# Performer query walk: key sums as stationary weights in 32-column groups, quotient made on channels

## The reference, cut to what matters

```python
qkv = x @ W_qkv                                   # q, k, v: (B, 12, 548, 16)
qf  = features(q, proj_mat, is_query=True)        # (B, 12, 548, 44)
kf  = features(k, proj_mat, is_query=False)
# features: ratio * (exp(dash - diag - stab) + 1e-4)
out = (qf @ (kf.T @ v)) / (qf @ kf.sum(tokens))   # numerator / denominator
h   = h + out @ W_proj + b_proj
```

## Time and profile before

| | us |
|---|---|
| median of 3 executions | 4794.83 |
| lowest, highest | 4787.97, 4799.33 |
| profiled execution, its own time | 4788.87 |
| span of the profiled execution | 4787.1 |
| granted TensorE clock, mean over the span | 0.977 |
| query walk, first product to last addition to X | 375.64 to 760.08 |

### The profile page before, as it was taken

One profiled execution on the slowest core, in us unless ns is written; L12 is line 12 of the kernel. 1 busy time (PEld: TensorE's weight loads), 2 busy tenths in 40 slices (PEclk: granted clock), 3 DMA queues, 4 the chain that ended last, 5 costly groups with the idle time before them and its releaser, 6 DMA issues. The chain is left out here.

```text
span 4787.1 us, 139366 instructions
## 1 busy us (share of the span) xinstructions
PE 4643.0 (97%) x57372; PEld 3836.4 (80%) x57372; DVE 2459.5 (51%) x7361; ACT 2203.3 (46%) x5115; POOL 1544.6 (32%) x2385
## 2 busy tenths in 40 slices
PE   6999998999979999999999999999999999899999
PEld 4667775666658888888888888888888888799998
DVE  5655554666645554555555455555545544352332
ACT  3443442555545555554554455455445445222444
POOL 1000002666643333333333333333333333000555
PEclk8999997999989999999999999999999999999999
DMA  4111110000000000000000000000000000232333
GB/s 107 22 36 40 37 29 6 1 1 2 1 13 2 13 2 13 20 13 2 13 13 2 13 13 13 2 13 13 2 13 13 13 2 13 66 90 71 64 66 55
DMA packets 123860, 110.63 MB, mean 23 GB/s; under 512 B 65480, under 2 KB 111901, under 8 KB 123237
## 3 DMA queue, kind: packets, MB, share of 16 engines
q1 hardware_dynamic: 96081, 66.76, 6.0%
q0 software_dynamic: 16528, 23.16, 2.7%
q10 hardware_dynamic: 10628, 11.80, 1.1%
HBM read 59.76 MB, written 41.48 MB: 21 GB/s over the span
## 5 line engine op out<-in xcount | busy, mean ns | idle before, releaser
L2139 PE MATMUL PS<-th_kT,th_qg 64*125 64x274 f32 x10560 | 1416.8, 400 | 0.0
L1856 POOL TENSOR_TENSOR th_qg<-th_qT,w_th_th 128x180 f32<-128x180 f32 x1760 | 848.0, 504 | 1629.8 <-PE PS L2139 1620.5
L2044 ACT ACTIVATE th_P<-PS 110x600 f32<-110x600 f32 x880 | 647.6, 736 | 1113.3 <-PE PS L2126 1113.3
L1962 DVE TENSOR_REDUCE th_nmx<-PS 125x1 f32<-125x548 f32 x880 | 641.2, 729 | 902.3 <-PE PS L2139 902.3
L2126 PEld LDWEIGHTS PS<-th_mixn,th_P 61*110 61x110 f32 x17600 | 979.6, 173 | 103.2 <-issue 25.0
L2139 PEld LDWEIGHTS PS<-th_kT,th_qg 64*125 64x125 f32 x10560 | 938.2, 184 | 142.5 <-issue 0.2
L2126 PE MATMUL PS<-th_mixn,th_P 61*110 61x60 f32 x17600 | 975.6, 254 | 2.1 <-ACT th_P L2044 1.8
L2054 ACT ACTIVATE th_P<-PS,th_nb 125x548 f32<-125x548 f32 x880 | 621.8, 707 | 106.7 <-DVE th_nb L1965 106.7
L1317 POOL TENSOR_SCALAR ga_P<-ga_P,ga_rw 110x110 f32<-110x110 f32 (+4 forms) x240 | 265.5, 1118 | 199.7 <-DVE ga_rw L1483 196.0
L2161 PEld LDWEIGHTS PS<-th_P,th_v 110*32 110x32 f32 x11520 | 245.5, 115 | 29.9 <-issue 28.9
L2161 PE MATMUL PS<-th_P,th_v 110*32 110x90 f32 (+1 forms) x11520 | 266.4, 253 | 2.2 <-issue 1.3
(11 more groups left out here) (345 smaller groups left out, 6318.3 us busy)
## 6 DMA issues: line engine op xcount, KB each, us to landing
pf_xT<-pf_spill SPq DMA_DIRECT2D x32, 412.5 KB, 5.4
ex_tokens<-th_xn SPq DMA_DIRECT2D x128, 82.5 KB
pf_spill<-pf_xT SPq DMA_DIRECT2D x16, 412.5 KB, 3.7
ex_turned<-th_rT SPq DMA_DIRECT2D x16, 412.5 KB, 3.1
ex_x<-ex_turned SPq DMA_DIRECT2D x32, 206.2 KB, 4.0
out_h<-X SPq DMA_DIRECT2D x16, 330.0 KB
ex_w<-in_L_ffn_W ACTq DMA_DIRECT2D x18, 288.0 KB
ex_w<-in_L_ffn_W ACTq DMA_DIRECT2D x8, 576.0 KB
```

The source lines that it names most:

```text
L1856: ins = pool.tensor_tensor(qg[:, m % SB, :, 64 * s:64 * s + HQ].rearrange("p c (h n) -> p c h n", n=QH), qT[:, im % 2, :, at + s * QH:at + ...
L1962: dve.tensor_reduce(nmx[:, p:p + 1], PS[0:MR, bank:bank + 2, 0:HK], AX.XY, ALU.max, negate=True) \
L2044: act.activation(P2[:, :, :, at * QT:(at + 1) * QT].rearrange("p t h (s n) -> p s (t h) n", s=2), PS[0:R, MB:MB + 2, 0:VO].rearrange("p s ...
L2139: ins = pe.matmul(PS[0:MR, bank + a, 0:HK], qg[s, p, c, 0:MR], kT[s, im % 2, c, :], start=c == 0, stop=c == NC - 1)
```

## The change

`numerators` now uses the key sums as stationary weights and the features `fT` as moving data. The sums are kept in two tiles: `kvn` (2 heads x 16 channels = 32 columns for each pair of heads, the numerators) and `kvd` (32 columns as well: the denominator column of each head repeated 16 times). A product has 32 weight columns and 110 moving columns and writes 32 partitions of the bank, group `g` of the columns of the array writing partitions 32g to 32g + 31. So numerators and denominators come out with channels on partitions and tokens on columns. `divide` makes the reciprocal of all repeated denominators (128 x 110 and 64 x 110) and multiplies them with the numerators, and writes `oT` directly. `turn_outputs` on PE and `outputs` on ACT are gone. `project` takes 128 and 65 rows in place of 96 and 97, and `wp` is laid out for that with one transfer more. The image's sums are made by two DVE instructions in place of one. The order of the calls within a step is changed on PE, ACT and DVE.

```diff
-                sp.dma_start(pf.wp[0:C], chunked(A["L0_attn_W_proj"])).then_inc(pf_in, 16)
-                sp.dma_start(pf.wp[C:C + 1, KC - 1, :], row(A["L0_attn_b_proj"])).then_inc(pf_in, 16)
+                sp.dma_start(pf.wp[:, 0, :], A["L0_attn_W_proj"][0:128]).then_inc(pf_in, 16)
+                sp.dma_start(pf.wp[0:D - 128, 1, :], A["L0_attn_W_proj"][128:D]).then_inc(pf_in, 16)
+                sp.dma_start(pf.wp[D - 128:D - 127, 1, :], row(A["L0_attn_b_proj"])).then_inc(pf_in, 16)
...
+        z = sb("z", [128, 2, R])
+        oT = sb("oT", [128, 2, 2, R])
...
-                pool.memset(oT[C:C + 1, :, :, :], 1.0).then_inc(filled, 1)
+                pool.memset(oT[REST:REST + 1, :, 1, :], 1.0).then_inc(filled, 1)
...
                 def divide(u):
                     if 0 <= u < NT:
-                        on = PS[0:R, NB, 0:H * HV].rearrange("p (h x) -> p h x", x=HV)
                         dve.wait_ge(num, u + 1)
-                        dve.reciprocal(zq[:, u % 2, :], on[:, :, HD]).then_inc(recip, 1)
+                        dve.reciprocal(z[:, 0, :], PS[:, NB, R:2 * R])
+                        dve.reciprocal(z[0:REST, 1, :], PS[REST:128, NB, 2 * R:3 * R]).then_inc(recip, 1)
                         dve.wait_ge(recip, u + 1)
                         if u >= 2:
-                            dve.wait_ge(oturn, u - 1)
-                        dve.tensor_tensor(o[:, u % 2, :].rearrange("p (h d) -> p h d", d=HD), on[:, :, 0:HD],
-                                          zq[:, u % 2, :].unsqueeze(2).broadcast_to([R, H, HD]), ALU.mult).then_inc(o_in, 1)
+                            dve.wait_ge(yprod, u - 1)
+                        dve.tensor_tensor(oT[:, u % 2, 0, :], PS[:, NB, 0:R], z[:, 0, :], ALU.mult)
+                        dve.tensor_tensor(oT[0:REST, u % 2, 1, :], PS[0:REST, NB, 2 * R:3 * R], z[0:REST, 1, :], ALU.mult) \
+                           .then_inc(oT_in, 1)
...
-                        dve.scalar_tensor_tensor(kv[:, i % 2], kvo[:, i], scale[0:2 * M, i:i + 1], vso[:, i], ALU.mult, ALU.add) \
+                        dve.scalar_tensor_tensor(pairs(kvn), parts(kvo)[:, :, :, 0:HD], scale[0:2 * M, i:i + 1],
+                                                 parts(vso)[:, :, :, 0:HD], ALU.mult, ALU.add)
+                        dve.scalar_tensor_tensor(pairs(kvd), sums(kvo), scale[0:2 * M, i:i + 1], sums(vso), ALU.mult, ALU.add) \
                            .then_inc(kvmade, 1)
                     if a < NT:
                         features(a)
-                        features(b)
                     divide(b - 4)
                     add(a - 4)
+                    if a < NT:
+                        features(b)
                     divide(a - 2)
                     add(b - 4)
...
                     if a < NT:
                         square(a)
-                        square(b)
-                    outputs(a - 4)
+                    features(a - 2)
                     if a < NT:
                         raise_queries(a)
-                    features(a - 2)
+                        square(b)
+                    features(b - 2)
                     if a < NT:
                         raise_queries(b)
-                    features(b - 2)
-                    outputs(b - 4)
...
                         if u >= 1:
-                            pe.wait_ge(o_in, u)
-                        for j in range(PAIRS):
-                            ins = pe.matmul(PS[0:R, NB, j * W34:(j + 1) * W34], fT[:, u % 2, j, :], kv[:, u // T % 2, j, :],
-                                            start=True, stop=True)
+                            pe.wait_ge(oT_in, u)
+
+                        def column(w, j, g, at):
+                            return pe.matmul(PS[32 * g:32 * g + 32, NB, at:at + R], w[:, u // T % 2, j * 32:(j + 1) * 32], fT[:, u % 2, j, :],
+                                             start=True, stop=True)
+
+                        for j in range(4):
+                            column(kvn, j, j, 0)
+                        for j in range(4):
+                            column(kvd, j, j, R)
+                        for j in range(2):
+                            column(kvn, 4 + j, j, 2 * R)
+                        for j in range(2):
+                            ins = column(kvd, 4 + j, 2 + j, 2 * R)
                         ins.then_inc(num, 1)
...
                 def project(u):
                     if 0 <= u < NT:
                         pe.wait_ge(oT_in, u + 1)
-                        for c in range(KC):
-                            ins = pe.matmul(PS[0:R, YB, 0:D], oT[0:kin(c), u % 2, c, :], wp[0:kin(c), c, :],
-                                            start=c == 0, stop=c == KC - 1)
-                        ins.then_inc(yprod, 1)
+                        if u >= 1:
+                            pe.wait_ge(xadd, u)
+                        pe.matmul(PS[0:R, YB, 0:D], oT[:, u % 2, 0, :], wp[:, 0, :], start=True, stop=False)
+                        pe.matmul(PS[0:R, YB, 0:D], oT[0:REST + 1, u % 2, 1, :], wp[0:REST + 1, 1, :], start=False, stop=True).then_inc(yprod, 1)
 
                 pe.wait_ge(vsown, B)
                 for s in range(STEPS + 2):
                     a, b = 2 * s, 2 * s + 1
                     if a < NT:
                         queries(a)
+                    numerators(b - 4)
+                    turn_features(a - 2)
+                    project(a - 4)
+                    if a < NT:
                         queries(b)
-                    turn_outputs(a - 4)
-                    turn_features(a - 2)
-                    numerators(b - 4)
-                    project(a - 4)
                     turn_features(b - 2)
-                    turn_outputs(b - 4)
                     numerators(a - 2)
                     project(b - 4)
```

More of the change, by code:

```diff
@@ L308, in _ @@
                 sp.wait_ge(text_in, 16 * (T + 1))
[L309 removed]
+                sp.wait_ge(pf_in, 16 * 7)
             @block.scalar
@@ L563, in performer @@
     TB, NB, YB = 4, 6, 7
+    REST = D - 128
     PW, HV = 2 * M + 1, HD + 1
@@ L591, in performer @@
         vso = sb("vso", [2 * M, B, PAIRS, W34])
-        kv = sb("kv", [2 * M, 2, PAIRS, W34])
+        kvn = sb("kvn", [2 * M, 2, PAIRS * 2 * HD])
+        kvd = sb("kvd", [2 * M, 2, PAIRS * 2 * HD])
         warm = sb("warm", [128, 16])
@@ L616, in performer @@
         qprod, qsq, qmax, qdiag, qadd, qsub, qexp = (sem(n) for n in ("qprod", "qsq", "qmax", "qdiag", "qadd", "qsub", "qexp"))
-        fturn, fT_in, kvmade, num, recip, o_in = (sem(n) for n in ("fturn", "fT_in", "kvmade", "num", "recip", "o_in"))
-        oturn, oT_in, yprod, xadd = (sem(n) for n in ("oturn", "oT_in", "yprod", "xadd"))
+        fturn, fT_in, kvmade, num, recip = (sem(n) for n in ("fturn", "fT_in", "kvmade", "num", "recip"))
+        oT_in, yprod, xadd = (sem(n) for n in ("oT_in", "yprod", "xadd"))
         STEPS = NT // 2
@@ L848, in _, with parts, pairs, sums @@
                             dve.wait_ge(num, T * (i - 1))
-                        dve.scalar_tensor_tensor(kv[:, i % 2], kvo[:, i], scale[0:2 * M, i:i + 1], vso[:, i], ALU.mult, ALU.add) \
+                        def parts(t):
+                            return t[:, i].rearrange("p j (a d) -> p j a d", d=HV)
+                        def pairs(t):
+                            return t[:, i % 2].rearrange("p (j a d) -> p j a d", a=2, d=HD)
+                        def sums(t):
+                            return parts(t)[:, :, :, HD:HV].broadcast_to([2 * M, PAIRS, 2, HD])
+                        dve.scalar_tensor_tensor(pairs(kvn), parts(kvo)[:, :, :, 0:HD], scale[0:2 * M, i:i + 1],
+                                                 parts(vso)[:, :, :, 0:HD], ALU.mult, ALU.add)
+                        dve.scalar_tensor_tensor(pairs(kvd), sums(kvo), scale[0:2 * M, i:i + 1], sums(vso), ALU.mult, ALU.add) \
                            .then_inc(kvmade, 1)
@@ L935, in features @@
                                        bias=eps[0:2 * M, :]).then_inc(fT_in, 1)
-                def outputs(u):
-                    if 0 <= u < NT:
-                        act.wait_ge(oturn, u + 1)
-                        if u >= 2:
-                            act.wait_ge(yprod, u - 1)
-                        act.activation(oT[0:C, u % 2], PS[0:C, YB, 0:KC * R].rearrange("p (c n) -> p c n", c=KC), ACT.Copy) \
-                           .then_inc(oT_in, 1)
                 for s in range(STEPS + 2):
```

12 lines of the change are left out of this document (1 added, 11 removed).

## The result

| | before | after |
|---|---|---|
| median of 20 executions each, us | 4797.39 | 4785.24 |
| lowest, highest | 4785.68, 4807.65 | 4772.25, 4800.17 |
| ratio, 95% interval | | 0.9979 [0.9969, 0.9989] |
| span of the profiled execution | 4787.1 | 4780.6 |
| mean granted clock | 0.977 | 0.975 |

A forecast was written before the change was run, and what follows sets the result against it. TensorE was taken to bound the kernel before. 36 steps falling from 9.41 to 8.71 us gain 25.2, less 4.4 for image sums: 20.8 off the median 4794.83 gives 4774.0 us, range 4756 to 4801.

The forecast's parts named there:

- the four column groups side by side: Numerators on TensorE: 24 MATMULs a tile overlap in four column groups, 0.74 us a tile against 1.10 before.
- TensorE's own step: TensorE's work in one walk step of two tiles: 8.36 us after the change, against 9.41 before.
- the loop over one bank: In the walk, each numerator waits for the previous tile's quotient, sharing one bank; this loop sets the step at 8.71 us.
- the place of TensorE's wait: TensorE waits about 0.35 us a step for VectorE's quotient, ahead of the numerators.
- serial column groups: Rival: the numerators' column groups don't overlap, 2.42 us for 0.74, 83 us lost, 4878; chance 0.07.
- dearer changes of mode: Rival: TensorE's tiling mode changes cost 0.35 us each for 0.17, step 9.6, time 4801; chance 0.05.
- the loose loop: Rival: the walk's waits are hidden, products cheaper; step floor 8.36 us, time 4760; chance 0.13.
- the dearer reciprocal: Rival: VectorE's reciprocals cost more and make it the bound; nothing gained from 8.2 ns a column, 4795; chance 0.17.
- x: What each of VectorE's four reciprocals a step costs above 0.84 us; from 0.20 nothing is gained.
- the plain step: Walk's steady part: 36 steps of two tiles fall from 9.41 to 8.71 us, 25.2 us gained.
- the image's sums: Two VectorE instructions for one, ahead of features(a): 0.29 us for each of 15 images, 4.4 us given back.
- head and tail: Walk's ends: same calls less two transposes, plus dearer quotients; taken as 0, between -1.5 and +1.5 us.

The follow-up runs named there:

- the packed kernel: Changed kernel with the last two head pairs' denominators in four column groups, one 128 x 165 reciprocal replacing two, second product cut in two: 4772.15, ratio 0.9954 to before.
- The idling runs: VectorE memsets added at the walk's end: changed kernel with one 4789.71 (0.9978), with two 4798.23 (0.9997); kernel before with two 4813.49 (1.0029).

## Why the prediction was right or wrong

**Right.** VectorE's long reciprocals were named as what decides, and copies in their place (ratio 0.9894) show it. Their price (840 ns for 835 and 847), the four column groups side by side (0.74 for 0.70 us a tile), TensorE's own step (8.36 for 8.29), the loop over one bank (8.71 for 8.75) and the place of TensorE's wait, ahead of the numerators, came as forecast (its size not: 0.64 a step for 0.35). Of the rivals, serial column groups and dearer changes of mode are excluded, the loose loop too, and the dearer reciprocal: x was 0.00. The Trainium skill's repeat count of 8 for the divide (VectorE: DVE Perf Modes, First, the fixed hardware budget) would by the prediction's estimate of eight cycles give 8.3 ns a column. The columns measured, up to 110 and 165, cost 6.2 to 6.3 each, and the measurement decides. (By that estimate a reciprocal of 110 columns is 1.05 us, not the 1.04 of the prediction.)

**Wrong: the size.** The step that failed is the sum, "36 x (9.41 - 8.71) = 25.2 gained, 4.4 given back: 20.8", carried unchanged to the time of the whole kernel. Term by term, in the walk:

| term | forecast | measured | from |
|---|---|---|---|
| the plain step | 25.2 | 23.8 | 36 x (9.41 - 8.75) |
| the image's sums | -4.4 | -6.6 | 321.59 - 36 x 8.75 |
| head and tail | 0 (± 1.5) | -2.3 | 24.80 + 23.19 against 23.59 + 22.13 |
| walk | 20.8 | 14.9 | 384.4 - 369.6 |

- The plain step: I let the second reciprocal start 0.09 before the first one's end, as the short reductions do. It starts 0.85 after the first (594.79, 595.64), with no overlap. That makes the quotient 0.09 longer; the part before it was 0.06 shorter, so that 8.75 for 8.71 is in part two errors that cancel. It is not the reciprocal's doing: the copies in its place did not overlap either, nor did the two halves of the second product in the packed kernel (0.43 us for two of 0.21). In all three pairs the second instruction reads the bank from partition 64 after one that read from partition 0; whether that is the reason was not tested.
- The sums: they take 0.66 a pair, as forecast 0.64. I took off 0.27 of slack and another 0.08 that VectorE would have had anyway. The longer quotients used the 0.08 up, and 0.25 of slack was there: 0.66 - 0.25 = 0.41 a pair, 0.39 by the run without them, so about 6 of the 6.6; the rest is not assigned.
- Head and tail lie outside their ± 1.5. In the tail every tile's numerators, quotient and projection follow each other with nothing to cover them, and the quotient is 1.5 us longer (2.17 for 0.27 + 0.36). Two transposes and a copy less pay for most of that, not all (+1.1). In the head (+1.2) the first numerators wait 2.54 us for a quotient, and the queries after them take 3.40 us for 2.07, at the lower clock for a part. The kernel before has such a stretch too, but of 3.4 us (from 388.0), where the changed one's is 6.8 (from 388.4).

```profile
388.71 0.59 PE L1051 MATMUL PS<-pf_fT,pf_kvn 88*32 88x110 f32 x8 [2.54 <-DVE pf_oT L836]
...
392.51 3.40 PE L1028 MATMUL PS<-w_pf_wQ,pf_xT 64*110 64x360 f32 x12
```

**Wrong: that the rest stays as it is.** The prediction took every microsecond of the walk as one of the kernel. The timed ratios give 10 (5 to 15) and 7 (0 to 13) of 14.9. The profiles show two places where it can be lost. One is the clock in the first 120 us of gated attention: 118.9 us twice for the changed kernel, 109.5 and 113.9 for the one before. The idling runs and the run without sums speak for the moment of the start there, from one profile each. The other is the 4.7 us in the stages behind, which go with the new form and not with the moment, and have no explanation. How the medians divide between the two stays open: the intervals are as wide as the effect, and gated attention as a whole took 642.1 and 653.8 us in two profiles of the same kernel.

## What to carry to other kernels

When work moves from the bound engine to one with room, make the sum for both and then for the loop between them. Terms that cost nothing while the other engine covered them (the image's sums) come back (here 0.4 of the 0.66 us of a pair), and slack can be spent only once. A reciprocal is paid by its columns (835 ns on 128 partitions and 847 on 64, for 110 columns), so spread it over all 128 partitions first: that took as much again off the walk here, 15.4 us, as the whole change, 14.9. And judge a gain of a few tenths of a per cent by timed runs and not by the stage that was changed: here the rest of the kernel took back about a third or more.

## What the runs showed of the hardware

- Reciprocal of f32 on VectorE: 216 ns for 10 columns, 835 for 110, 1184 for 165, 6.2 to 6.3 ns a column beyond the ten, the same from PSUM and for 64 or 128 partitions. Two that are independent start 0.85 us apart at 0.84 us each, and two copies in their place 0.28 apart at 0.26, where the products behind them, 0.27 long, start 0.19 apart.
- Products with 32 weight columns in four column groups: 24 MATMULs of 110 columns in 0.70 us, 29 ns each, one change of mode included.
- TensorE's clock fell to its lower level in 23 of 37 steps where the engine waited 1.8 us at a time for VectorE (24 MATMULs in 4.8 to 6.4 us for 3.88), and stayed full in the steady part of the changed kernel, where they were mostly 0.4 and 0.6 and at most 1.0.
- Gated attention, the same code in every run, took 631 to 654 us, with the granted clock of its third 40 us between 0.64 and 0.91. The stages behind it took 3390.2 to 3393.9 us in four profiles with the old form and 3394.5 to 3399.8 in ten with the new one.
